# Key and attention-output transposes as pairs of 64-row tiles beside the scores, in a cosformer and mixture-of-experts block

## The chip, the cores and the metric

One core of one Trainium2 chip runs the whole program in one launch. The metric is the device time of that core in microseconds. The kernel is written engine by engine: each engine has its own list of instructions and waits on semaphores that other engines raise.

## What is computed

The input is x, 2048 tokens of 128 numbers. The reference, cut to what matters here:

```python
# x: (1, 2048, 128); 16 heads of 64
n = layernorm(x)
Q, K, V = n @ Wq + bq, n @ Wk + bk, n @ Wv + bv
Qp, Kp = relu(Q), relu(K)
Qc, Qs = Qp * cos, Qp * sin        # angle = pi / (2 * 2048) * token
Kc, Ks = Kp * cos, Kp * sin
# token by token, for each head (a causal linear attention):
S_cos += Kc outer V;  S_sin += Ks outer V;  z_cos += Kc;  z_sin += Ks
out = (Qc @ S_cos + Qs @ S_sin) / max(Qc . z_cos + Qs . z_sin, 1e-6)
x = x + out @ Wo + bo
n = layernorm(x)
# eight experts, the best two for each token, 128 -> 512 -> 128 with gelu
x = x + sum over the two experts of softmax weight * expert(n)
```

## The kernel before

The 2048 tokens are cut into 16 tiles of 128 tokens. Four tiles (`SC`) make one group, and the groups `i` = 0 to 3 (`NS` = 4) run one after another, each as a **front** and an **attention**; behind the last one comes the stage of the experts with 39 blocks.

**The front** (`front`, L1064) computes, with the normed tokens turned so that features lie on partitions, 16 blocks (`block(j)`: eight for keys, eight for queries; three matmuls each, L1054 to L1056) and eight halves of the values (`values(m)`, after the blocks named in `V_AT`). ScalarE takes each block out of PSUM with a relu into `kT` or `qT` (L570). VectorE takes each half of the values out (L712) and writes it twice into `vcs`, times cosine and sine (L716). Between these VectorE also does small steps of the group before: the second layer norm (L789 to L808), and the choice of the two experts (`best_two`, L817 to L838). Then it masks the first scores (`masked(i, 0)`, L751), behind `best_two` in its order and ahead of the last half of the values.

`kT` holds two heads of 64 features on 128 partitions for eight pairs of heads. The keys are needed with tokens on partitions as well (`kn`), for the update of the state. So the front also has eight **key jobs** (`keys(m)`, L1089): each turns four 128x128 squares of `kT` into PSUM bank 5 (L1099), and ScalarE copies the bank to `kn` (L561). `K_AT` says ahead of which block each job stands; the last one stands behind `values(7)`. There are 4 groups x 8 jobs x 4 = 128 such transposes.

**The attention** (L1262) walks over eight pairs `p` of head groups (two pairs for each tile). For each p TensorE does `scores(i, p)` (L1135: eight matmuls with 64 rows each, the two halves of the rows in two PSUM banks), then `outputs(i, p - 1)`: `before` (L1152: queries against the state, 64 rows each, 64x128 tiles) and `within` (L1173 and L1180, 128x64 tiles). An ordinary fp32 matmul of this kernel shows in the trace as two records with a weight load each, a transpose as one. VectorE masks the scores (`masked`) and takes state and outputs away (`taken`, L761 and L767) once ScalarE has copied the sums (`out_sums`, L598). TensorE waits in `scores(p)` for the mask of p-1 (`am_ok`), and in `before(n)` for `tcs_ok` of group n-2.

When a tile is complete, VectorE makes the reciprocal of the denominator (L774), GpSimd divides (`normalise`, L432) into `on`, TensorE turns `on` (`turn_out`, L1193, eight 128x128 transposes, banks 6 and 7, L1200), ScalarE copies to `oT` (L553), and `project` (L1209) multiplies by Wo into bank 7; VectorE adds that to the residual (`residual`, L779). `turn_out` of tiles 0, 1, 2 stands behind `outputs` at p = 3, 5, 7; that of tile 3 stands in the next front (behind block 3), for the last group in the stage of the experts.

Banks 6 and 7 also hold other things for a while: the gate's logits (bank 7, `gate`, L1222, read at L817), the ranks (bank 6, read by `places`, L854), and in the last attention the table of blocks (`blocks_before`, `block_table`, `match_blocks`, `table`) and the first rows for the experts (`first_rows`, `turn_y`).

## Time and profile before

| what | value |
|---|---|
| median of three runs | 376.09 us (376.0 to 377.35) |
| profiled execution, its own time | 377.03 us |
| its span, first to last instruction | 375.2 us |
| granted TensorE clock, mean over the span | 0.985 |
| TensorE busy | 351.7 us (94%) |
| VectorE / ScalarE / GpSimd busy | 65% / 42% / 35% |

A matmul's record lasts longer than the step to the next one, since matmuls are pipelined. The price of a piece of TensorE work is therefore read from starts to starts in the timeline, not from record lengths. In the timeline one row merges consecutive records of one kind: start, length, what, count, and in brackets the idle time of the engine ahead of it with who ended it.

### The profile page before, as it was taken

How to read it: one execution, taken by the hardware profiler on the slowest of the kernel's cores; microseconds unless marked ns; L12 is line 12 of the kernel's file. 1: busy time of each engine (PE TensorE's matmuls, PEld its weight loads, DVE VectorE, ACT ScalarE, POOL GpSimd, SP SyncE). 2: the span in 40 equal slices, each digit the busy share in tenths (PEclk: the TensorE clock that was granted, in tenths of full speed). 3: DMA queues.
4: the chain of work that ended last, by engine and by line, in shares of the span. 5: the costliest groups of instructions: out<-in, count | busy, mean ns of one | idle time of the engine just before them, and what ended most of it. 6: DMA issues, size and time to landing. Idle time of an engine off the chain costs nothing.

```text
span 375.2 us, 10993 instructions
## 1 busy us (share of the span) xinstructions
PE 351.7 (94%) x4125; PEld 319.0 (85%) x4125; DVE 244.9 (65%) x774; ACT 156.5 (42%) x369; POOL 130.1 (35%) x130
## 2 busy tenths in 40 slices
PE   7999999999999999999999999999899999999920
PEld 7877999888899988889898888999789899999910
DVE  4889665768966566896646679866656554444515
ACT  4773231467222146622214672212345555555510
POOL 4022522212086320207732030455037675444530
PEclk9999999999999999999999999999999999999985
DMA  7941530531001000000100005300646677667129
GB/s 254 309 206 40 229 136 10 210 128 52 9 24 48 18 2 1 0 9 27 41 17 9 3 0 145 98 27 26 171 126 191 186 206 213 187 192 192 35 60 282
DMA packets 32773, 38.65 MB, mean 103 GB/s; under 512 B 4140, under 2 KB 25025, under 8 KB 31697
## 3 DMA queue, kind: packets, MB, share of 16 engines
q1 hardware_dynamic: 27248, 31.90, 27.5%
q0 software_dynamic: 2272, 4.46, 3.5%
q10 hardware_dynamic: 3200, 1.58, 1.4%
q8 instruction: 34, 0.56, 0.6%
q14 instruction: 19, 0.15, 0.1%
HBM read 22.91 MB, written 15.47 MB: 102 GB/s over the span
## 4 chain that ended last, share of the span: by engine, by line
PE 82%; DVE 5%; DMA 5%; issue 3%; POOL 1%; ACT 1%; SPq 1%; ACTq 0%; DVEq 0%; POOLq 0%
PE ps L1135 9%; PE ps L1173 9%; PE ps L1359 8%; PE ps L1344 8%; PE ps L1152 7%; PE ps L1180 7%; PE ps L1209 7%; PE ps L1054 6%; PE ps L1056 5%; PE ps L1055 5%; PE ps L1200 4%; PE ps L1099 3%; DMA zin<-zbuf 2%; PE ps L1331 1%; DMA ident<-c_ident 1%
## 5 line engine op out<-in xcount | busy, mean ns | idle before, releaser
L598 ACT ACTIVATE os<-ps 128x260 f32<-128x260 f32 x64 | 24.9, 389 | 99.8 <-PE ps L1180 99.8
L639 ACT ACTIVATE hT<-ps,b1t 128x128 f32<-128x128 f32 x156 | 44.6, 369 | 38.6 <-PE ps L1344 38.6
L474 POOL DMA_INDIRECT ybuf<-yr,slot x32 | 31.9, 997 | 69.4 <-DVE yr L846 31.7
L432 POOL TENSOR_TENSOR on<-tcs,rden 128x1024 f32<-128x1024 f32 x16 | 30.4, 1903 | 65.0 <-DVE rden L774 65.0
L512 POOL DMA_INDIRECT zbuf<-z,tokens x39 | 38.0, 975 | 31.1 <-DVE z L997 25.6
L761 DVE TENSOR_TENSOR state<-ps,state 128x260 f32<-128x260 f32 x64 | 27.4, 428 | 32.4 <-ACT os L598 30.1
L751 DVE TENSOR_TENSOR am<-ps,pair 128x1024 f32<-128x1024 f32 x32 | 38.7, 1208 | 9.3 <-issue 6.7
L1359 PE MATMUL ps<-w_sb,hT 128*128 x312 | 43.1, 281 | 0.6 <-DVE zs L993 0.4
L1344 PE MATMUL ps<-xb,w1b 128*128 128x128 f32 x312 | 42.3, 278 | 0.0
L1173 PE MATMUL ps<-vcs,am 128*64 128x65 f32 x1024 | 42.2, 225 | 0.0
L1173 PEld LDWEIGHTS ps<-vcs,am 128*64 128x64 f32 x1024 | 36.8, 137 | 3.9
L1180 PE MATMUL ps<-vcs,kn 128*64 128x130 f32 x512 | 39.5, 275 | 0.0
L1359 PEld LDWEIGHTS ps<-w_sb,hT 128*128 128x128 f32 x312 | 37.8, 191 | 1.9 <-issue 1.4
L1135 PE MATMUL ps<-qT,kT 64*128 64x128 f32 x512 | 37.2, 284 | 1.0 <-DVE am L751 0.9
L1344 PEld LDWEIGHTS ps<-xb,w1b 128*128 128x128 f32 x312 | 37.9, 192 | 0.0
L1135 PEld LDWEIGHTS ps<-qT,kT 64*128 64x128 f32 x512 | 31.2, 187 | 6.9 <-issue 6.2
L716 DVE TENSOR_SCALAR vcs<-os,cs 128x512 f32<-128x512 f32 x64 | 32.6, 552 | 1.1
L1152 PE MATMUL ps<-state,qT 64*128 64x130 f32 x480 | 33.3, 277 | 0.0
L1209 PE MATMUL ps<-wo_sb,oT 128*128 128x128 f32 x256 | 31.6, 278 | 0.0
L712 DVE TENSOR_TENSOR os<-ps,bv_all 128x512 f32<-128x512 f32 x32 | 22.0, 689 | 14.6 <-PE ps L1056 14.6
L1209 PEld LDWEIGHTS ps<-wo_sb,oT 128*128 128x128 f32 x256 | 29.8, 192 | 1.7 <-issue 1.4
L1152 PEld LDWEIGHTS ps<-state,qT 64*128 64x128 f32 x480 | 30.2, 187 | 0.8 <-issue 0.7
(121 smaller groups left out, 590.0 us busy)
## 6 DMA issues: line engine op xcount, KB each, us to landing
w1b<-in_L_ffn_w SPq DMA_DIRECT2D x39, 256.0 KB, 2.9
ybuf<-blank SPq DMA_DIRECT2D x8, 1152.0 KB, 4.6
yb<-ybuf SPq DMA_DIRECT2D x39, 72.0 KB, 2.9
w_sb<-in_L_ffn_w SPq DMA_DIRECT2D x8, 256.0 KB
x_sb<-in_L_attn_x SPq DMA_DIRECT2D x4, 256.0 KB, 5.2
pair<-c_pair SPq DMA_DIRECT2D x16, 64.0 KB, 2.3
zin<-zbuf SPq DMA_DIRECT2D x4, 256.0 KB, 4.8
zin<-zbuf ACTq DMA_DIRECT2D x4, 256.0 KB, 5.3
```

The lines of the kernel that those rows point to most:

```text
L474: pool.indirect_dma_start(ybuf, bass.IndirectOffsetOnAxis(ap=slot[:, k, c:c + 1], axis=0), yr[:, k, c, :], None).then_inc(y_out[u], 16)
L512: pool.indirect_dma_start(zbuf, bass.IndirectOffsetOnAxis(ap=tokens[:, b:b + 1], axis=0), z[:, b % ZR, :], None, bounds_check=2 * T - 1, o ...
L639: act.activation(hT[:, b % 2, f, :], ps[:, b % 2 * 2 + f // 2, f % 2 * P:f % 2 * P + P], ACT.Gelu, bias=b1t[:, b % XR, f:f + 1]).then_inc( ...
L716: last = dve.tensor_scalar(vcs[:, m // 2, (m % 2) * 8:(m % 2) * 8 + 8, s, 0:DH], vb[:, m % 2, :].rearrange("p (h d) -> p h d", d=DH), cs4[ ...
L751: dve.tensor_tensor(am[:, p % 2, :, :, :], ps[:, 0:2, :].rearrange("p r (q t) -> p r q t", t=P), pair[:, c, None, None, :].broadcast_to([P ...
L1135: last = mm(ps[:, r, b * P:(b + 1) * P], kT[rows, of, c * P:(c + 1) * P], qT[rows, of, c * P:(c + 1) * P], start=True, stop=True)
L1152: mm(ps[:, 2 + 2 * (n % 2) + r, 0:2 * CS].rearrange("p (s b v) -> p b s v", s=2, b=2)[:, q, :, :], qT[rows, 2 * g + q, c * P:(c + 1) * P], ...
L1173: mm(ps[t:t + 64, 2 + 2 * (n % 2) + r, q * VW:q * VW + VW], am[:, n // 2 % 2, r, (2 * g + q) % (PH // 2), t:t + 64], vcs[:, c, g * GH + 2 ...
L1180: last = mm(ps[64 * r:64 * r + 64, 2 + 2 * (n % 2) + q, 2 * CS:3 * CS], kn[:, c, (2 * g + q) * P + r * DH:(2 * g + q) * P + (r + 1) * DH], ...
L1209: last = mm(ps[:, 7, at:at + D], oT[:, c % 2, pr, :], wo_sb[:, pr, :], start=(pr == 0), stop=(pr == NP - 1))
L1344: last = mm(ps[:, b % 2 * 2 + f // 2, f % 2 * P:f % 2 * P + P], w1b[b % WR][:, f * P:(f + 1) * P], xb[:, b % XR, :], start=True, stop=True ...
L1359: last = mm(ps[:, z_bank(b), 0:D], hT[:, b % 2, f, :], w, start=(f == 0), stop=(f == FB - 1))
```

## The change

`turn_out` and the key jobs use 64x128 row tiles in place of whole 128x128 squares. A transpose of 64 partitions by 128 columns has 64 columns of the identity as its moving side. Two of them, on partitions 0 to 63 and 64 to 127, stand in pairs and write different banks.

- `turn_out(c)`: 16 half transposes in eight pairs (tokens 0 to 63 into bank 6, 64 to 127 into bank 7). It moves behind `scores` at p = 4, 6, 8, ahead of `outputs(p - 1)`; at p = 8 there are no scores. For tile 3 its place is kept. The wait for the residual (`x2_ok`) now stands ahead of both banks.
- `keys(i, c)`: one job for each tile, 16 half transposes in eight pairs. Tile 0 is turned at the end of the front, behind `scores(i, 0)` (banks 5 and 7, behind a wait for `lg_ok` when bank 7 held logits); tiles 1, 2, 3 inside the attention behind `scores` at p = 2, 3, 5 (banks 6 and 7). The copies on ScalarE follow: still eight of 512 columns for each group, two at the end of the front and six in the attention, ahead of `out_sums(2p - 2)`.
- New or moved waits of TensorE are in the diff. On VectorE, `residual`, and in the last group `match_blocks` and `table`, move ahead of `masked` of the same p.
- In the last group, `block_table` moves from p = 6 to the end of p = 5, and `first_rows` with `turn_y` from ahead of `outputs(7)` to between its `before` and its `within`.

```diff
+KEYS_AT = {2: 1, 3: 2, 5: 3}
+TURN_AT = {4: 0, 6: 1, 8: 2}
+def key_bank(c, r):
+    return 5 + 2 * r if c == 0 else 6 + r
...
 # ScalarE, attention
-                    if g == 2 and c >= 1:
-                        turn_out(i, c - 1)
+                    if n % 2 == 0 and n // 2 + 1 in TURN_AT:
+                        turn_out(i, TURN_AT[n // 2 + 1])
+                    if n % 2 == 0 and n // 2 + 1 in KEYS_AT:
+                        keys(i, KEYS_AT[n // 2 + 1])
                     out_sums(i, n)
...
 # VectorE, attention
-                    masked(i, p)
                     if p % 2 == 1 and p > 4:
...
+                    masked(i, p)
+                    if tail and p == 1:
+                        places(i - 1)
...
 # TensorE, end of the front
                 scores(i, 0)
+                if tail:
+                    pe.wait_ge(lg_ok, i)
+                keys(i, 0)
                 values(V_JOBS - 1)
-                keys(K_JOBS - 1)
...
+            def keys(i, c):
+                for pr in range(NP):
+                    for r in range(2):
+                        rows = slice(HT * r, HT * r + HT)
+                        last = pe.transpose(ps[:, key_bank(c, r), pr * DH:pr * DH + DH], kT[rows, pr, c * P:(c + 1) * P],
+                                            ident[rows, rows])
...
                 for n in (2 * p, 2 * p + 1):
                     if not opening:
                         before(i, n)
+                if i == NS - 1 and p == PAIRS - 1:
+                    pe.wait_ge(oT_ok, i * 2 * SC + 2 * (SC - 2) + 1)
+                    first_rows()
+                    pe.wait_ge(oT_ok, i * 2 * SC + 2 * (SC - 1))
+                    turn_y(i, 7)
                 for n in (2 * p, 2 * p + 1):
                     within(i, n, opening)
...
             def turn_out(i, c):
                 pe.wait_ge(on_ok, i * SC + c + 1)
-                for half in range(2):
-                    if half == 1 and c >= (1 if i == NS - 1 else 2):
-                        pe.wait_ge(x2_ok, i * SC + c)
-                    for q in range(4):
...
+                if c >= (1 if i == NS - 1 else 2):
+                    pe.wait_ge(x2_ok, i * SC + c)
+                for pr in range(NP):
+                    for k in range(2):
+                        rows = slice(HT * k, HT * k + HT)
+                        last = pe.transpose(ps[:, 6 + k, pr * HT:pr * HT + HT],
+                                            on[rows, c % 2, 2 * pr:2 * pr + 2, :].rearrange("p h d -> p (h d)"),
+                                            ident[rows, rows])
...
 # TensorE, attention, behind scores(i, p)
+                    if p in KEYS_AT:
+                        if p == 2 and tail:
                             pe.wait_ge(cnt_ok, i + 1)
+                        if p == 3:
+                            pe.wait_ge(kn_ok, i * K_JOBS + 4)
+                        if p == 5:
+                            pe.wait_ge(oT_ok, i * 2 * SC + 2)
                         if p == 5 and i == NS - 1:
                             pe.wait_ge(match_ok, 1)
+                            pe.wait_ge(x2_ok, i * SC + 1)
+                        keys(i, KEYS_AT[p])
+                    if p in TURN_AT:
+                        if p < PAIRS:
+                            pe.wait_ge(kn_ok, i * K_JOBS + (6 if p == 4 else 8))
+                        if p == 6 and i == NS - 1:
+                            pe.wait_ge(tab_ok, 1)
...
+                        turn_out(i, TURN_AT[p])
+                    outputs(i, p - 1, opening=not tail and p <= 2)
+                    if p == 5 and i == NS - 1:
+                        pe.wait_ge(kn_ok, i * K_JOBS + K_JOBS)
+                        block_table(0)
```

## Rows read from the trace of the kernel before

**Rows 1.** The page, part 1: busy time, share of the span, instructions.

```profile
PE 351.7 (94%) x4125; PEld 319.0 (85%) x4125; DVE 244.9 (65%) x774; ACT 156.5 (42%) x369; POOL 130.1 (35%) x130
```

**Rows 2.** Waits of TensorE: us in total, times, longest.

```profile
PE ps L1135 <- DVE am L751: 0.9, 1, 0.9
```

**Rows 3.** Groups by line and shape: busy us, mean ns of one record.

```profile
L1099 PE MATMUL ps<-ident,kT 128*128 128x128 f32 x128 | 19.3, 273 | 0.1
...
L1173 PEld LDWEIGHTS ps<-vcs,am 128*64 128x64 f32 x1024 | 36.8, 137 | 3.9
L1099 PEld LDWEIGHTS ps<-ident,kT 128*128 128x128 f32 x128 | 15.7, 142 | 3.4 <-issue 0.5
L1222 PEld LDWEIGHTS ps<-gate_sb,yT 128*128 128x128 f32 x32 | 4.2, 191 | 0.3
```

**Rows 4.** Timeline of TensorE, third front, around two key jobs.

```profile
147.97 0.60 PE L1099 MATMUL ps<-ident,kT 128*128 128x128 f32 x4
...
148.65 0.39 PE L1055 MATMUL ps<-xT_lo,W 128*128 128x512 f32 x1
148.88 0.39 PE L1056 MATMUL ps<-xT_hi,W 128*128 128x512 f32 x1
...
150.49 0.60 PE L1099 MATMUL ps<-ident,kT 128*128 128x128 f32 x4
```

**Rows 5.** Chain of work in order of time, second attention: start, us, what.

```profile
105.02 1.09 PE ps L1135 x16
106.11 0.97 PE ps L1152 x16
107.08 0.62 PE ps L1173 x16
107.69 0.45 PE ps L1180 x8
108.14 0.47 PE ps L1173 x16
...
109.05 1.02 PE ps L1200 x8
110.08 1.09 PE ps L1135 x16
```

**Rows 6.** Timeline of TensorE, fourth front, the gate's matmuls and what follows.

```profile
224.62 0.95 PE L1222 MATMUL ps<-gate_sb,yT 128*128 128x8 f32 x8
225.43 0.64 PE L1099 MATMUL ps<-ident,kT 128*128 128x128 f32 x4
```

**Rows 7.** Timeline of VectorE, third front.

```profile
147.47 0.69 DVE L712 TENSOR_TENSOR os<-ps,bv_all 128x512 f32<-128x512 f32 x1 [0.62 <-PE ps L1056]
...
149.99 0.69 DVE L712 TENSOR_TENSOR os<-ps,bv_all 128x512 f32<-128x512 f32 x1 [0.41 <-PE ps L1056]
...
155.94 0.69 DVE L712 TENSOR_TENSOR os<-ps,bv_all 128x512 f32<-128x512 f32 x1 [0.70 <-PE ps L1056]
...
158.46 0.69 DVE L712 TENSOR_TENSOR os<-ps,bv_all 128x512 f32<-128x512 f32 x1 [0.92 <-PE ps L1056]
...
161.94 1.22 DVE L751 TENSOR_TENSOR am<-ps,pair 128x1024 f32<-128x1024 f32 x1
```

**Rows 8.** Timeline of VectorE, first front: its last idle time and the first mask.

```profile
19.83 0.69 DVE L712 TENSOR_TENSOR os<-ps,bv_all 128x512 f32<-128x512 f32 x1 [0.92 <-PE ps L1056]
...
31.21 1.21 DVE L751 TENSOR_TENSOR am<-ps,pair 128x1024 f32<-128x1024 f32 x1
```

**Rows 9.** Timeline of ScalarE, last attention: one copy of turned outputs.

```profile
253.60 1.09 ACT L553 ACTIVATE oT<-ps 128x512 f32<-128x512 f32 x2 [0.19 <-PE ps L1200]
```

**Rows 10.** Timeline of TensorE, end of the last attention.

```profile
264.23 1.09 PE L1200 MATMUL ps<-ident,on 128*128 128x128 f32 x8
...
266.73 0.33 PE L1259 MATMUL ps<-ident,yb 128*128 128x128 f32 x1 [0.83 <-DMA yb<-ybuf]
...
267.20 1.17 PE L1152 MATMUL ps<-state,qT 64*128 64x130 f32 x16
```

More of the change, by code:

```diff
@@ L50 @@
 K_JOBS = 2 * SC
+HT = P // 2
 GROUPS = SC * NG
@@ L916, in attention @@
                             residual(i, 0, 2)
-                    if tail and p == 1:
-                        places(i - 1)
                     if i == NS - 1 and p == 5:
@@ L1087, in values @@
                            ).then_inc(v_ps, 1)
-                def keys(m):
-                    c, half = K_ORDER[m]
-                    if m == 0:
-                        pe.wait_ge(big_ok, i * QK_JOBS + NP // 2)
-                    elif half == 1:
-                        pe.wait_ge(big_ok, i * QK_JOBS + NP)
-                    if m >= 1:
-                        pe.wait_ge(kn_ok, i * K_JOBS + m)
-                    for q in range(4):
-                        last = pe.transpose(ps[:, 5, q * P:(q + 1) * P], kT[:, half * 4 + q, c * P:(c + 1) * P], ident[:])
-                    last.then_inc(kn_ps, 1)
                 for j in range(QK_JOBS):
@@ L1104, in front @@
                         pe.wait_ge(tcs_ok, i * GROUPS)
-                    if j in K_AT:
-                        keys(K_AT[j])
                     block(j)
@@ L1118, in front @@
                 scores(i, 0)
+                if tail:
+                    pe.wait_ge(lg_ok, i)
+                keys(i, 0)
                 values(V_JOBS - 1)
-                keys(K_JOBS - 1)
                 if tail:
@@ L1137, in scores, with keys @@
                 last.then_inc(sc_ps, 1)
+            def keys(i, c):
+                for pr in range(NP):
+                    for r in range(2):
+                        rows = slice(HT * r, HT * r + HT)
+                        last = pe.transpose(ps[:, key_bank(c, r), pr * DH:pr * DH + DH], kT[rows, pr, c * P:(c + 1) * P],
+                                            ident[rows, rows])
+                        if pr == NP - 1:
+                            last.then_inc(kn_ps, 1)
             def before(i, n):
@@ L1143, in before @@
                     pe.wait_ge(v_add, i * V_JOBS + V_JOBS)
-                    pe.wait_ge(kn_ok, i * K_JOBS + K_JOBS)
+                    pe.wait_ge(kn_ok, i * K_JOBS + 2)
                 if n >= 2:
@@ L1162, in within @@
                     pe.wait_ge(v_add, i * V_JOBS + V_JOBS)
-                    pe.wait_ge(kn_ok, i * K_JOBS + K_JOBS)
+                    pe.wait_ge(kn_ok, i * K_JOBS + 2)
                 if opening and n >= 2:
@@ L1194, in turn_out @@
                 pe.wait_ge(on_ok, i * SC + c + 1)
-                for half in range(2):
-                    if half == 1 and c >= (1 if i == NS - 1 else 2):
-                        pe.wait_ge(x2_ok, i * SC + c)
-                    for q in range(4):
-                        pr = half * 4 + q
-                        last = pe.transpose(ps[:, 6 + half, q * P:(q + 1) * P],
-                                            on[:, c % 2, 2 * pr:2 * pr + 2, :].rearrange("p h d -> p (h d)"),
-                                            ident[:])
-                    last.then_inc(oT_ps, 1)
+                if c >= (1 if i == NS - 1 else 2):
[6 more added lines that the diff above has]
+                                            ident[rows, rows])
+                        if pr == NP - 1:
+                            last.then_inc(oT_ps, 1)
             def project(i, c):
@@ L1287, in attention @@
                             blocks_before(0)
-                        if i == NS - 1 and p == 6:
-                            pe.wait_ge(tab_ok, 1)
                         if i == NS - 1 and p == PAIRS:
```

29 lines of the change are left out of this document (6 added, 23 removed).

## The prediction, made before the change was built

> **What bounds the kernel now.** I read the busy times first, then who waited for whom, then the timelines of TensorE and VectorE side by side through one front, one attention and the last attention. TensorE is busy 94% of the span, and no other engine comes near [rows 1]. The list of its waits has hardly anything in it: the largest one inside the groups is a single 0.9 us at the first mask of the first front [rows 2]. So from the second group on every piece of TensorE work lies on the path, and a piece that gets shorter shortens the kernel, unless an engine close behind TensorE then becomes the last. The question is therefore twofold: what a transpose costs in either form, and who stands close behind TensorE in the stretch that loses work. Over the span VectorE is busy only 65% [rows 1], but in the fronts it has almost no holes: in the third front, from the second layer-norm step to the first mask, only three holes, 0.41, 0.70 and 0.92 us [rows 7]; in the first front none at all after 19.83 [rows 8].
>
> **Price of the whole transposes.** From one key job to the next but one piece in the third front it is 2.52 us (147.97 to 150.49). In it stand nine projection matmuls with 0.23 us from start to start, 2.10 us. So a job of four costs 0.42 us and one whole transpose 0.105 us [rows 4]. A `turn_out` in the attention costs 1.03 us (109.05 to 110.08) [rows 5], against 8 x 0.105 = 0.84 in a run of whole tiles; the other 0.19 us I take as the price of one more change of tile form (128x64 to 128x128 to 64x128 instead of straight from the first to the last). All in all 128 transposes of keys [rows 3] and as many of outputs.
>
> **Price of the pairs, t for a job of eight pairs.** No half transpose is in the trace, so I bound it. From below: half the moving columns at the whole price, 0.105 / 2 a pair, t = 0.42. Nearest row: `within` in its second half, 16 records with 65 moving columns on pairs of 64-column tiles, in 0.47 us, 0.029 us a record [rows 5]; t = 0.46 to 0.47. That row tiles overlap in pairs is seen in the scores: 16 records with 128 moving columns in 1.09 us, 0.068 each, form change included, which is well below 0.105 for the same columns in a whole tile [rows 5]. From above, by the weight load: the gate's eight records have only 8 moving columns and still take 0.81 us (224.62 to 225.43), so an ordinary load of 128 columns takes 0.10 us [rows 6], and with two loads side by side t = 0.81. Further above, if the halves follow one another at the whole price: 16 x 0.105, t = 1.68. I take t = 0.46. The load's record decides: the transposes' loads last 142 ns, as long as those of 64 columns (137), not as the gate's (191), though all 128 columns are loaded [rows 3]; so their load is the short kind, and `within` shows what pairs with short loads cost.
>
> The Trainium skill speaks against this choice: "TensorE: Matmul & The Clock Gate", section "LDWEIGHTS (loading the stationary operand)", says that a load's time follows its columns and not its rows, so a half transpose, still 128 columns wide, would load as long as a whole one. The gate's row agrees with it for ordinary loads; the 142 ns of the transposes' loads speak against applying it here. By that rule the sum would be that of the second rival below.
>
> **The fronts.** Eight key jobs leave each front (8 x 0.42 = 3.36 us of TensorE), one job t comes back, and the front's `turn_out` becomes t plus a form change in and out, 0.66 in place of 0.84. TensorE alone would gain about 3.1 us. But VectorE sets the end. From the third value half (147.47) to the seventh (158.46) it runs 10.99 us with 2.03 us of holes, 8.96 of work [rows 7]. The third half itself comes earlier by one key job and the `turn_out`'s 0.2: 0.6 us. Without holes the seventh half is taken 0.6 + 2.03 = 2.6 us earlier; TensorE's part of it (six key jobs and 0.2: 2.7) is just in time. After that VectorE works without a hole (multiplications, `best_two`, mask) to the end of the first mask, and `scores(1)` waits for it. So a tail front gains 2.6 us less a little for semaphores: 2.55, three times, **7.7 us**. `keys(0)` at its end costs nothing there: TensorE has 0.5 us to spare before `scores(1)`; without this cover it costs t, 0.46, each. The wait for `lg_ok` stands before `keys(0)`, with `values(7)` and the ranks queued behind it; VectorE copies the logits right after the seventh half, while `scores(0)` runs for 1.1 us, so I cost it at nothing (a tenth or two if late, inside the same 0.5). In the **first front** VectorE is without a hole from 19.83 to the mask at 31.21 [rows 8], and TensorE waits 0.9 us for it already [rows 2]. Only the two key jobs ahead of the fourth half count: **0.8 us**; the rest turns into waiting.
>
> **The attentions.** In each, three `turn_out` change from 1.03 to t and three key jobs of t come in: 3 x (1.03 - 2t), with t = 0.46 a gain of 0.33, four times **1.3 us**. The moved copies of the keys on ScalarE: the present copies of two banks start 0.19 us after the transposes and last 1.09 [rows 9]; the sums that stand behind them are due after `before` and one `within`, 0.97 + 0.62 + 0.45 = 2.04 us [rows 5]. 0.76 us to spare, so I cost them at nothing; without that cover each of the 24 jobs would hold up `out_sums`, `taken` and then `before`. The waits on `kn_ok`, `oT_ok`, `cnt_ok`, `on_ok` and the earlier `x2_ok` each ask for something that ended a `scores` or an `outputs` before, with the half transposes and `outputs` queued behind. The wait for GpSimd's division gets looser, as tile 0 is turned a `scores` later. `residual` ahead of `masked` on VectorE waits for `project`, which TensorE ended before the very scores that `masked` needs: nothing.
>
> **The last attention.** `turn_out(1)` now waits for the table, with `outputs(5)` behind it; VectorE writes the table after both `taken` of p = 5, so one `scores` (about 1 us) has to cover what an `outputs` covered. Bounds 0 to 1 us; I take 0.4. The other way `first_rows` behind `before` hides the copy and the load that it waited for: up to 0.83 + 0.25 us of the stretch 264.23 to 267.20 [rows 10], though `before(15)` now meets `taken(13)`; I take 0.4. Together nothing. The table is finished earlier, but SP's first loads also wait for the scattered rows, whose place is kept. `turn_out(3)` behind it saves 0.84 - 0.66 and a little: **0.3 us**.
>
> **Sum.** 7.7 + 0.8 + 1.3 + 0.3 = 10.1 us; as a function of t: 24t - 21.2. The profiled execution took 377.03, 0.9 above the median; 10.1 less is 366.9 for it, and **366.0** beside the median of 376.09. The experts' stage starts earlier as a whole and keeps its own pace, for TensorE is the bound there too.
>
> **The rivals.**
> First, ScalarE's copies become late. They are written in pieces of 64 numbers instead of in one run. If two copies took 2.2 us instead of 1.09, they would pass the 2.04 us by 0.33, 24 times: 8 us, 374. It decides from 1.85 us. For it: no copy of this shape is in the trace. Against it: the 0.76 us to spare, and the sums themselves are not awaited at once. Partly right it gives 369 to 373.
> Second, the pair is bound by its loads, t = 0.81 as by the gate's row: 24 x 0.81 - 21.2 = -1.8, 374.3, and up to 375.5 where a form change adds 0.05 a job. This is no measurable change, or just below it.
> Third, on the slower side: two half transposes don't overlap at all and each costs what a whole one costs, 0.105: t = 1.68, +19 us, 395. It decides where 24t passes 21.2, at t = 0.88, 0.055 us a half one after another or 0.11 a pair. For it: no transpose in row pairs is in the trace. Against it: the scores' and the queries' records in the same form overlap [rows 5].
>
> **How the numbers follow.** Forecast (t from 0.42 to 0.6, fronts bound by VectorE): 0.70, 363 to 369. Late copies: 0.11, 369 to 374. Bound by loads: 0.11. Serial halves: 0.08. The range 362.5 to 373 takes the forecast's bounds (t = 0.42 gives 365.0, and the 0.55 us of each tail front that I gave to VectorE would bring 363.3) and most of the late copies, and leaves out the loads' case and the serial one. About 0.5%, 1.9 us, is what a measurement here tells from no change: faster (below 374.2) 0.81, within 0.11, slower 0.08.
>
> **What would show it.** Eight pairs in 0.42 to 0.6 us between `scores` and `before` in the timeline; at 0.8 the loads bind. Fronts shorter by 2.5 us, with a new wait of TensorE for the mask (L751) of up to 0.5 us at the end of each, and of over 2 us in the first. Copies of keys on ScalarE of about 0.55 us each, ended before the sums. Attentions shorter by about 0.3 us. The prediction is wrong if a job takes over 0.7 us, if TensorE waits for `tcs` or ScalarE in the attention, or if the fronts shrink by far less than 2 us.

## The result, and the profile after

The changed kernel takes 371.54 us (median of 4, 370.48 to 373.75) against 376.72 for the kernel before, measured beside it: a ratio of 0.9872 with a 95% interval of 0.9844 to 0.990, or 1.3% faster. A later set of the same kernel (`after_again`, expected near 371.5) gave 372.85 (median of 6, 371.01 to 373.95), ratio 0.9894 [0.987, 0.9919]. The forecast was 366.0. The direction was right and the time lies in the range, but the gain is 5.2 us where 10.1 were worked out: half of it is missing. The time also lies above the 363 to 369 of the forecast itself, in the part of the range that was kept for late copies on ScalarE. These did not come, as is shown below, so it is luck that the time fell inside the range.

The profiled execution took 372.44 us, its span is 370.6. From its page: busy time of the engines, the granted clock in 40 slices, and the shares of the chain that ended last. PE is TensorE, PEld its weight loads, DVE VectorE, ACT ScalarE and POOL GpSimd.

```profile
PE 342.9 (93%) x4381; PEld 309.7 (84%) x4381; DVE 244.5 (66%) x774; ACT 157.3 (42%) x369; POOL 129.9 (35%) x130
...
PEclk9998999999999999999999999999999999999975
...
PE 74%; DVE 12%; DMA 4%; issue 4%; POOL 2%; ACT 2%; SPq 1%; ACTq 0%; DVEq 0%; POOLq 0%
```

TensorE is busy 8.8 us less than in [rows 1] although the span shrank by only 4.6. The rest became waiting. The chain says the same: VectorE holds 12% of it, where it held 5% before. And one slice near the start of the clock row reads 8. The list of TensorE's waits (who waited <- for whom, us in total, times, longest) stands against a single 0.9 inside the groups in [rows 2]:

```profile
PE ps L1128 <- DVE am L757: 3.6, 5, 2.0
...
PE ps L1137 <- issue: 0.9, 1, 0.9
...
PE ps L1208 <- POOL on L438: 0.7, 1, 0.7
PE ps L1155 <- DVE tcs L773: 0.5, 1, 0.5
...
PE ps L1208 <- issue: 0.3, 1, 0.3
```

L1128 is the scores, L1137 the keys, L1208 `turn_out`, L1155 `before`, L757 the mask; `issue` means that the profile shows nothing that was waited for. The one wait of `before` in this list stands in the last attention (262.89); those of the groups before it lie inside merged rows. Where in the program this lies is read from the starts of landmarks on TensorE (first block of a front, second scores of a group, first hidden matmul of the experts), the same in both timelines:

| stage, us | before | after | forecast | measured |
|---|---|---|---|---|
| first front, to `scores(1)` | 22.97 | 22.31 | -0.8 | -0.66 |
| fronts 2, 3, 4, each | 26.18 | 23.72 | -2.55 | -2.46 |
| attention 1 | 38.19 | 40.26 | -0.33 | +2.07 |
| attention 2, 3, each | 40.18 | 40.53 | -0.33 | +0.35 |
| attention 4, to the experts | 42.49 | 44.20 | -0.33 | +1.71 |
| start, and the experts' stage with tile 3 | 112.64 | 111.60 | -0.3 | -1.04 |

The last row moves by as much between kernels that don't touch it (the experts' stage 102.15 to 103.67, the start 9.2 to 11.3), so nothing is read into it. The fronts came out as forecast. The attentions were to give 1.3 us and took 4.5: the whole error is there.

**The price of a job.** Timeline of TensorE in the second attention of the changed kernel (start, us, what):

```profile
108.61 1.16 PE L1128 MATMUL ps<-qT,kT 64*128 64x128 f32 x16
109.60 0.66 PE L1208 MATMUL ps<-ident,on 64*128 64x64 f32 x16
110.09 1.12 PE L1155 MATMUL ps<-state,qT 64*128 64x130 f32 x16
...
113.12 1.16 PE L1128 MATMUL ps<-qT,kT 64*128 64x128 f32 x16
114.11 0.66 PE L1137 MATMUL ps<-ident,kT 64*128 64x64 f32 x16
114.61 1.12 PE L1155 MATMUL ps<-state,qT 64*128 64x130 f32 x16
```

From start to start a job of eight pairs takes 0.49 to 0.50 us (109.60 to 110.09, 114.11 to 114.61), 0.062 a pair. So t = 0.50, where 0.46 was taken. The step from scores to scores is 4.51 with either job in it, where the kernel before has 5.06 with a whole `turn_out` [rows 5] and, by the same trace, 3.96 to 4.04 without.

**The end of a front.** The third one, TensorE:

```profile
156.50 1.16 PE L1128 MATMUL ps<-qT,kT 64*128 64x128 f32 x16
...
157.50 0.66 PE L1137 MATMUL ps<-ident,kT 64*128 64x64 f32 x16
...
159.87 1.16 PE L1128 MATMUL ps<-qT,kT 64*128 64x128 f32 x16 [0.36 <-DVE am L757]
```

`keys(0)` stands inside the time that TensorE had to spare, and what is left of that, 0.36 us, is the new wait for the mask. The mask itself starts 22.36 us after the front's first block (158.51), against 24.82 in [rows 7]. In the first front the same wait is 2.01 us, where it was 0.93.

### The profile page after: what moved, and what is told of

Same layout as the page of the kernel before. It is cut to its first block, busy times and chain, and to the rows that moved or that the text cites. A ratio compares the mean times of both kernels' runs of the same rounds, so it can differ in the third digit from the quotient of the medians.

```text
span 370.6 us, 11502 instructions
## 1 busy us (share of the span) xinstructions
PE 342.9 (93%) x4381; PEld 309.7 (84%) x4381; DVE 244.5 (66%) x774; ACT 157.3 (42%) x369; POOL 129.9 (35%) x130
## 2 busy tenths in 40 slices
DMA packets 32774, 38.68 MB, mean 104 GB/s; under 512 B 4139, under 2 KB 25024, under 8 KB 31696
## 3 DMA queue, kind: packets, MB, share of 16 engines
q10 hardware_dynamic: 3200, 1.58, 1.4%
## 4 chain that ended last, share of the span: by engine, by line
PE 74%; DVE 12%; DMA 4%; issue 4%; POOL 2%; ACT 2%; SPq 1%; ACTq 0%; DVEq 0%; POOLq 0%
PE ps L1357 9%; PE ps L1372 8%; PE ps L1176 8%; PE ps L1128 7%; PE ps L1218 7%; PE ps L1183 7%; PE ps L1155 6%; PE ps L1060 5%; PE ps L1062 5%; PE ps L1061 5%; DVE vcs L722 2%; PE ps L1344 2%; PE ps L1208 2%; DMA zin<-zbuf 2%; DVE am L757 2%
## 5 line engine op out<-in xcount | busy, mean ns | idle before, releaser
L1176 PE MATMUL ps<-vcs,am 128*64 128x65 f32 x1024 | 42.9, 227 | 0.0
L1372 PE MATMUL ps<-w_sb,hT 128*128 x312 | 41.9, 278 | 0.6 <-DVE zs L999 0.5
L1128 PE MATMUL ps<-qT,kT 64*128 64x128 f32 x512 | 37.3, 285 | 3.6 <-DVE am L757 3.6
L1183 PE MATMUL ps<-vcs,kn 128*64 128x130 f32 x512 | 40.4, 279 | 0.0
L1128 PEld LDWEIGHTS ps<-qT,kT 64*128 64x128 f32 x512 | 31.3, 188 | 9.9 <-issue 8.8
L757 DVE TENSOR_TENSOR am<-ps,pair 128x1024 f32<-128x1024 f32 x32 | 38.6, 1207 | 0.9 <-PE ps L1128 0.8
L1155 PE MATMUL ps<-state,qT 64*128 64x130 f32 x480 | 34.5, 279 | 0.9 <-DVE tcs L773 0.5
L1155 PEld LDWEIGHTS ps<-state,qT 64*128 64x128 f32 x480 | 29.9, 188 | 1.7 <-DVE tcs L773 1.7
L574 ACT ACTIVATE kT<-ps,bcols 128x512 f32<-128x512 f32 x32 | 21.6, 689 | 19.8 <-PE ps L1062 19.7
```

The source lines that it names most:

```text
L757: dve.tensor_tensor(am[:, p % 2, :, :, :], ps[:, 0:2, :].rearrange("p r (q t) -> p r q t", t=P), pair[:, c, None, None, :].broadcast_to([P ...
L1128: last = mm(ps[:, r, b * P:(b + 1) * P], kT[rows, of, c * P:(c + 1) * P], qT[rows, of, c * P:(c + 1) * P], start=True, stop=True)
L1155: mm(ps[:, 2 + 2 * (n % 2) + r, 0:2 * CS].rearrange("p (s b v) -> p b s v", s=2, b=2)[:, q, :, :], qT[rows, 2 * g + q, c * P:(c + 1) * P], ...
L1176: mm(ps[t:t + 64, 2 + 2 * (n % 2) + r, q * VW:q * VW + VW], am[:, n // 2 % 2, r, (2 * g + q) % (PH // 2), t:t + 64], vcs[:, c, g * GH + 2 ...
L1183: last = mm(ps[64 * r:64 * r + 64, 2 + 2 * (n % 2) + q, 2 * CS:3 * CS], kn[:, c, (2 * g + q) * P + r * DH:(2 * g + q) * P + (r + 1) * DH], ...
L1372: last = mm(ps[:, z_bank(b), 0:D], hT[:, b % 2, f, :], w, start=(f == 0), stop=(f == FB - 1))
```

## The experiments

The theory formed from this: t = 0.50 explains 24 x 0.04 = 0.96 of the 5.8 us that the attentions are off; the rest is four waits or their consequences. (1) After the 2.01 us wait of the first front the granted clock falls, and the first attention runs slowly for a while, 1.6 us. (2) At p = 8 `before(15)` now meets a wait that the long `turn_out(2)` had covered, 0.48 in each of the first three groups. (3) and (4) In the last attention VectorE stands still behind GpSimd at p = 3 and p = 5, ahead of the mask: 0.60 and 1.09. The rivals blame the half transposes themselves or their places. Line numbers are those of each kernel, so they are shifted by some lines in places. Medians of the kernel before, measured beside the experiments, lie at 376.55 to 376.91. The fronts behind the first one are called tail fronts.

### A filler in the first front's wait

The slow stretch of attention 1: timeline of TensorE in the changed kernel, then its busy time by stretch (us, busy and count for PE, PEld, DVE, ACT, POOL, then granted clock, DMA share, GB/s).

```profile
31.63 1.16 PE L1128 MATMUL ps<-qT,kT 64*128 64x128 f32 x16 [2.01 <-DVE am L757]
...
36.14 1.08 PE L1128 MATMUL ps<-qT,kT 64*128 64x128 f32 x12
```

```profile
32.00:35.50 3.50, 3.50 (x59) 3.38 (x58) 2.66 (x6) 0.39 (x1) 0.00 (x0) 0.65 0.05 16
...
35.50:39.00 3.50, 3.50 (x71) 3.10 (x68) 2.19 (x4) 1.73 (x4) 0.00 (x0) 0.86 0.83 337
39.00:60.00 21.00, 21.00 (x427) 19.64 (x424) 13.99 (x30) 8.27 (x19) 7.04 (x7) 1.00 0.31 123
```

The step from `scores(1)` to `scores(2)` is 4.51 us, 3.07 in the kernel before. Mean clocks of 0.65 and 0.86 are full speed and the lower of the two levels, 1.2 GHz, mixed (0.51 from 33 to 36 us). The edit fills the wait with eight matmuls that no one reads (work that the kernel itself uses ahead of its start), in a bank that is free:

```diff
                 if tail:
                     ranks(i - 1)
+                else:
+                    keep_busy(8, 6)
...
```

> The changed kernel with eight matmuls on zeros into bank 6 put in front of the first group's scores(1), where TensorE waits 2.01 us for the first mask. Theory 'idle time costs the clock': the granted clock stays at 1.00 from 30 to 40 us (it was 0.51 from 33 to 36), the step from scores(1) to scores(2) of the first attention goes from 4.51 to about 3.1 us, the one after it from 3.70 to 3.56, and the time is about 370.8 us or 1.6 below the disturbed profile of the changed kernel (372.4). Rival 'the half transposes at 28 us bring the clock down': they stand in the same place here, so the clock falls again and the step stays at 4.5.

Measured (`e1_filler`): 371.02 (370.45 to 372.19), ratio 0.9842 [0.9816, 0.9868]. The same stretches of this kernel:

```profile
32.00:35.50 3.50, 3.26 (x67) 2.92 (x68) 3.27 (x7) 0.40 (x2) 0.00 (x0) 1.00 0.02 5
35.50:39.00 3.50, 3.50 (x82) 3.26 (x82) 2.65 (x6) 2.15 (x5) 0.00 (x0) 1.00 0.72 287
```

The wait shrinks to 0.24, the clock stays at 1.00, the first step is 3.07 again and attention 1 takes 38.68: 1.58 less. The front is as long as before (22.33), since VectorE sets its end. So in these two profiles the waiting itself was free and the clock after it was not. The medians differ by less, 0.5 us, and their intervals overlap: by their mean clocks, the clock does not fall in every execution. The four of the changed kernel took 372.44, 373.75, 370.48 and 370.65 us at mean clocks of 0.977, 0.976, 0.981 and 0.982.

### The first front without the statistics of two groups

VectorE computes the first layer norm's statistics of groups 1, 2 and 3 in the first front. Those of 2 and 3 move into the first attention, and GpSimd's roots of them with them:

```diff
-                    if not tail and 4 <= m < NS + 3:
-                        norm1_stats(m - 3)
+                    if not tail and m == 4:
+                        norm1_stats(1)
...
+                    if i == 0 and p in (3, 4):
+                        norm1_stats(p - 1)
...
```

> The changed kernel with the layer-norm statistics of token groups 2 and 3 taken out of the first front on VectorE (two pieces of 1.47 us) and put behind the state updates of p = 3 and p = 4 in the first attention. Theory 'VectorE sets the end of the first front': scores(1) comes 2.8 us after the start of scores(0) plus its own work, the wait for the mask falls from 2.01 us to under 0.3, the two waits of 0.22 and 0.57 for the value halves vanish, the clock stays at 1.00, in all 2.8 + 1.6 = 4.4 us less: 368 us. Rival 'another engine stands right behind it' (ScalarE's relus): the wait shrinks by less than 1 us and the time by under 1.5 us.

Measured (`e2_stats_late`): 369.21 (369.03 to 372.9), ratio 0.9831 [0.9774, 0.9887]; 368 was expected. The first front takes 20.14, 2.17 less, of some 2.8 us that left VectorE there. So VectorE set the end of that front. Now TensorE does, for the first mask waits 0.30 us for the scores:

```profile
28.10 1.23 DVE L763 TENSOR_TENSOR am<-ps,pair 128x1024 f32<-128x1024 f32 x1 [0.30 <-PE ps L1136]
```

TensorE's wait for the first mask is gone and the clock stays at 1.00. Attention 1 takes 39.59, not 38.68: GpSimd takes one of the moved roots right ahead of a division (48.46 and 49.43), and the step that holds `turn_out(1)`, which needs this division, is 9.62 in place of 8.72.

### Whole transposes again at p = 8

```diff
+                if i < NS - 1 and c == SC - 2:
+                    for pr in range(NP):
+                        last = pe.transpose(ps[:, 6 + pr // 4, pr % 4 * P:pr % 4 * P + P],
+                                            on[:, c % 2, 2 * pr:2 * pr + 2, :].rearrange("p h d -> p (h d)"), ident[:])
...
```

> The changed kernel with tile 2 of the groups 0 to 2 turned by eight whole transposes again, at its new place (p = 8, without scores ahead). Theory 'at p = 8 the shorter job only uncovers the wait for the state sums': the job gets about 0.5 us longer three times, the wait inside before() shrinks by as much, from scores(7) to the next front stays 9.8 us (it was 9.86 with whole tiles before the change, 9.81 after), and the time does not move (under 0.4 us). Rival, the prediction's sum: each of the three jobs counts in full, 3 x 0.5 = 1.6 us more and 10.3 us for the stretch.

Measured (`e3_whole_at_p8`): 372.49 (370.45 to 374.61), ratio 0.9886 [0.9844, 0.9929]. Its executions spread like those of the changed kernel, so the medians, 0.95 us apart, decide nothing here; the stretch does. From `scores(7)` to the next front it takes 9.86, against 9.81 in the changed kernel and 9.86 in the kernel before. `turn_out(2)` costs 1.02 in this form:

```profile
130.26 1.09 PE L1211 MATMUL ps<-ident,on 128*128 128x128 f32 x8
131.28 1.17 PE L1159 MATMUL ps<-state,qT 64*128 64x130 f32 x16
```

This is 0.45 us more than in the changed kernel (66.05 to 66.62), and the stretch is only 0.05 longer. What the half form saves at this place is waited away at once. The changed kernel's rows at p = 8 of the first group, of TensorE, of the weight loads of `before`'s second half, and of VectorE's step that takes outputs 13:

```profile
66.05 0.71 PE L1208 MATMUL ps<-ident,on 64*128 64x64 f32 x16
66.62 1.56 PE L1155 MATMUL ps<-state,qT 64*128 64x130 f32 x16
68.11 0.69 PE L1176 MATMUL ps<-vcs,am 128*64 128x65 f32 x16
...
67.46 0.53 PEld L1155 LDWEIGHTS ps<-state,qT 64*128 64x128 f32 x8 [0.31 <-DVE tcs L773]
...
66.94 0.47 DVE L773 SCALAR_TENSOR_TENSOR tcs<-os,cs,ps 128x260 f32<-128x260 f32 x1
```

`before` takes 1.49 us there and 1.05 where nothing holds it up (110.09 to 111.14), 0.44 of the 0.48 that the stretch lost: in its second half it waits until VectorE has taken outputs 13 (until 67.41). At the other p a `scores` of 1 us stands between; at p = 8 there is none, only `turn_out`. In the kernel before, `before` took 1.09 at this place (132.25 to 133.34): the whole `turn_out` covered the wait.

### The last attention's table steps, reordered

VectorE has a few tiny steps of the experts' table ahead of masks. Its rows in the last attention, first VectorE, then GpSimd (POOL), then TensorE:

```profile
234.77 1.75 DVE L882 SCALAR_TENSOR_TENSOR ex<-nq,small,free 128x2 fp32r<-128x2 f32 x1
236.44 1.21 DVE L757 TENSOR_TENSOR am<-ps,pair 128x1024 f32<-128x1024 f32 x1
...
244.69 0.15 DVE L891 SCALAR_TENSOR_TENSOR early<-ps,ex 128x2 f32<-128x2 f32 x1
244.88 1.25 DVE L894 TENSOR_TENSOR free<-free,early 128x2 f32<-128x2 f32 x1
...
246.20 1.21 DVE L757 TENSOR_TENSOR am<-ps,pair 128x1024 f32<-128x1024 f32 x1
```

```profile
234.60 1.90 POOL L438 TENSOR_TENSOR on<-tcs,rden 128x1024 f32<-128x1024 f32 x1 [0.71 <-DVE rden L780]
...
244.21 1.90 POOL L438 TENSOR_TENSOR on<-tcs,rden 128x1024 f32<-128x1024 f32 x1 [0.71 <-DVE rden L780]
```

```profile
237.70 1.16 PE L1128 MATMUL ps<-qT,kT 64*128 64x128 f32 x16 [0.53 <-DVE am L757]
...
246.38 0.71 PE L1137 MATMUL ps<-ident,kT 64*128 64x64 f32 x16 [0.91 <-issue]
```

L882 and L894 touch two numbers a row and take 1.75 and 1.25 us. Both end when GpSimd's division ends: 234.77 + 1.75 = 236.52 and 234.60 + 1.90 = 236.50; 244.88 + 1.25 and 244.21 + 1.90, 246.13 and 246.11. L891, between them, reads PSUM for one input and takes 0.15. The Trainium skill, "SBUF — State Buffer", section "Who interferes with whom", says that a VectorE instruction with two inputs in SBUF contends with a GpSimd instruction that reads SBUF, and calls such contention an exclusive lock; the trace agrees with these numbers. The mask behind each step is late by that much, and TensorE with it: `scores(4)` by 0.53, and `keys(3)`, which asks for the table's match (L895), by 0.91. The stand-still at p = 3 is no child of the change (the kernel before has one of 1.75 us at 239.84), but there a `turn_out` stood between it and the scores. The one at p = 5 is new: in the kernel before the same step came behind the mask and behind the end of the division (250.75), and took 0.16 us:

```profile
251.68 0.16 DVE L888 TENSOR_TENSOR free<-free,early 128x2 f32<-128x2 f32 x1
```

There TensorE also asked for the match an `outputs` later, at `turn_out(1)` and not at `keys(3)`.

First only VectorE's order is changed. `full_blocks` goes behind the mask of p = 3, and the update of `free` (L894) from ahead of the match to behind the mask of p = 5:

```diff
+                    if i == NS - 1 and p == 3:
+                        full_blocks(0)
+                    if i == NS - 1 and p == 5:
+                        early_out(0)
...
-                    if i == NS - 1 and p == 2:
-                        full_blocks(0)
```

> The changed kernel with two small steps of VectorE in the last attention put later: full_blocks(0) behind the mask of p = 3 instead of ahead of it, and the update of the free blocks (1.25 us while GpSimd divides) behind the match and the mask of p = 5. Theory 'small steps on VectorE that read only SBUF stand still until GpSimd has ended its division, and now stand ahead of what TensorE waits for': the wait of scores(4) (0.53) goes to under 0.1 and the one of keys(3) (0.91 in the list) to under 0.2, about 1.3 us less in the last attention (44.2 to 42.9). Rival 'the match itself stands still too' (it also reads two SBUF tiles): keys(3) waits as long as now, only 0.5 us are gained.

Measured (`e4_table_order`): 370.23 (369.98 to 374.91), ratio 0.9831 [0.9804, 0.9858]. The step from `scores(3)` to `scores(4)` fell from 5.11 to 4.51, as expected; that at p = 5 only from 5.82 to 5.69, and attention 4 takes 43.36 where 42.9 was expected: there the rival was right. VectorE and GpSimd of this kernel:

```profile
246.11 1.39 DVE L893 SCALAR_TENSOR_TENSOR match<-small,ps,ex 128x17 f32<-128x17 f32 x1
247.42 1.21 DVE L757 TENSOR_TENSOR am<-ps,pair 128x1024 f32<-128x1024 f32 x1
```

```profile
245.57 1.90 POOL L438 TENSOR_TENSOR on<-tcs,rden 128x1024 f32<-128x1024 f32 x1 [0.71 <-DVE rden L780]
```

Now the match stands still, until 247.50 (the division ends at 247.47). It has one input in PSUM and two in SBUF, 0.23 us without company. So the order on VectorE alone was not the cause at p = 5. The division beside it is left, and the next run moves it.

### GpSimd's division behind the match

`full_blocks` as above, `free` where it was, and one wait more on GpSimd in the last group:

```diff
                 pool.wait_ge(rden_ok, i * SC + c + 1)
+                if i == NS - 1 and c == 1:
+                    pool.wait_ge(match_ok, 1)
...
```

> The changed kernel with full_blocks(0) behind the mask of p = 3, and GpSimd's division of tile 1 in the last group held back until the match is written (TensorE needs that division only at p = 6). Theory 'VectorE's small steps with two SBUF inputs stand still until GpSimd's division has ended': the match is done 0.5 us after residual(0), the wait of keys(3) falls from about 0.8 to under 0.2 us, the step from scores(5) to scores(6) from 5.8 to about 4.9, the last attention from 44.2 (43.4 with the first part alone) to about 42.6; nothing else moves. Rival 'keys(3) waits for the residual or the copies, not the match': the step stays at 5.7.

Measured (`e4b_divide_after_match`): 369.22 (368.97 to 370.26), ratio 0.9801 [0.9768, 0.9833]. VectorE's match and mask, then GpSimd's division:

```profile
242.88 0.24 DVE L897 SCALAR_TENSOR_TENSOR match<-small,ps,ex 128x17 f32<-128x17 f32 x1
243.44 1.22 DVE L759 TENSOR_TENSOR am<-ps,pair 128x1024 f32<-128x1024 f32 x1 [0.33 <-PE ps L1130]
```

```profile
243.27 1.90 POOL L440 TENSOR_TENSOR on<-tcs,rden 128x1024 f32<-128x1024 f32 x1 [1.84 <-DVE match L897]
```

The match takes 0.24 us, the mask behind it waits for the scores, the step at p = 5 is 4.73, with 0.18 of `block_table` in it (5.82 in the changed kernel), and attention 4 takes 42.18, 2.02 less than in the changed kernel. This settles (3) and (4).

It also tells something of (1): here the wait in the first front is 2.0 us as well, but the granted clock of 32 to 39 us is 1.00 and attention 1 takes 38.68. In two more profiles on the same chip (`e5_rows_apart`, `e6_whole_moved`) the wait is 1.7 us and the clock stays too. In the four other profiles with the 2.0 us wait (the changed kernel twice, `e3_whole_at_p8`, `e4_table_order`) it fell; in the six with a wait of at most 0.93 it never did. Four of these six (`e1_filler`, `e2_stats_late`, `e8_all_three`, `e9_block_early`) ran on chips where it fell behind the long wait. In these runs, then, the fall comes only behind the long wait, and not always; whether the chip or the moment decides was not tried.

### GpSimd's opening of the residual behind its first division

If VectorE sets the end of the tail fronts, as the prediction had it, work of GpSimd that slows VectorE there must cost the front time. `open_residual` leaves the front:

```diff
+                    if i >= 1:
+                        rows_paced(i, c)
+                    normalise(i, c)
                     if c == 0:
...
                         open_residual(i)
-                    if i >= 1:
-                        rows_paced(i, c)
-                    normalise(i, c)
```

> The changed kernel with GpSimd's addition of the output bias to the tokens (1.28 us, in the fronts) put behind its first division in each attention. Theory 'VectorE sets the end of the tail fronts, and GpSimd stretches two of its multiplications there from 0.88 to 1.97 us': these take about 0.9 to 1.4 (the copy of 0.61 us still stands beside them), VectorE is ready about 0.6 to 1.1 us earlier, TensorE's wait for the mask (0.36 us) vanishes and the front falls from 23.72 to about 23.3: about 1.2 us in three fronts. Rival 'TensorE sets the end of the front': no change.

Measured (`e7_open_late`): 370.01 (369.57 to 370.66), ratio 0.9817 [0.9786, 0.9847]. The first front takes 21.23, 1.08 less, with a wait of 0.9 and the clock at 1.00. But the tail fronts take 23.69, only 0.03 less, and the wait for the mask stays at 0.37: there the theory fell. VectorE's sixth and seventh value halves, in the third front, have holes ahead of them again:

```profile
150.53 0.69 DVE L718 TENSOR_TENSOR os<-ps,bv_all 128x512 f32<-128x512 f32 x1 [0.62 <-PE ps L1062]
152.63 0.69 DVE L718 TENSOR_TENSOR os<-ps,bv_all 128x512 f32<-128x512 f32 x1 [0.48 <-PE ps L1062]
```

In the tail fronts of this kernel TensorE sets the time up to the seventh value half, and VectorE only from there to the mask. In the changed kernel VectorE has no hole there, and its seventh half starts at the same point of the front (18.87 us behind the first block, 18.85 here): both engines arrive together. The prediction's two sums for that stretch, 2.6 by VectorE and 2.7 by TensorE, were so close that either gave the right number.

### The halves not in pairs

Both loops are swapped, so that eight halves of partitions 0 to 63 come first and then eight of 64 to 127:

```diff
-                for pr in range(NP):
-                    for r in range(2):
+                for r in range(2):
+                    for pr in range(NP):
```

> The changed kernel with the same 16 half transposes of every job in another order: first the eight of partitions 0 to 63, then the eight of 64 to 127, so that neighbours share their rows of the array. Theory 'a pair costs 0.06 us because its two halves run side by side': a job goes from 0.50 to 0.85 or more (16 x 0.053), the steps of 4.51 between scores become about 4.9, the time grows by about 7 us. Rival 'the halves follow one another in any case and are simply short': the job stays at 0.50.

Measured (`e5_rows_apart`), one execution: 377.41. The rows between which a job lies:

```profile
109.94 1.16 PE L1128 MATMUL ps<-qT,kT 64*128 64x128 f32 x16
...
114.74 1.16 PE L1128 MATMUL ps<-qT,kT 64*128 64x128 f32 x16
```

The step is 4.80, 0.30 more than with pairs, so a job costs 0.80: 0.050 us for each half after another, 0.062 for a pair. Half transposes overlap when partitions and banks alternate, but by 0.30 of 0.80 and not by half. This order changes both at once, so which of the two counts is not shown. A single half costs half of a whole one (0.105, [rows 4]), not as much. Without the pairing no gain is left (377.41 against 376.91 for the kernel before).

### Whole transposes at the new places

The places of the change with 128x128 squares, in `keys`, `turn_out` and ScalarE's copies:

```diff
                 for pr in range(NP):
-                    for k in range(2):
-                        rows = slice(HT * k, HT * k + HT)
...
+                    last = pe.transpose(ps[:, 6 + pr // 4, pr % 4 * P:pr % 4 * P + P],
+                                        on[:, c % 2, 2 * pr:2 * pr + 2, :].rearrange("p h d -> p (h d)"), ident[:])
```

> The changed kernel with whole 128x128 transposes in all key and output jobs, everything at its new place. Theory 'only the form makes the new places pay': a job beside the scores costs 0.84 + about 0.2 to 0.35 for two more changes of form, 1.05 to 1.2 us instead of 0.50, the steps of 4.51 become 5.1 to 5.2; five such jobs in each attention are not covered by a wait: 4 x 5 x 0.6 = 12 us more than the changed kernel, slower than before the change by 6. Rival 'the new places alone give the gain': as fast as the changed kernel within 2 us.

Measured (`e6_whole_moved`), one execution: 384.19. The rows of one job and its neighbours:

```profile
112.00 1.16 PE L1127 MATMUL ps<-qT,kT 64*128 64x128 f32 x16
113.09 1.09 PE L1203 MATMUL ps<-ident,on 128*128 128x128 f32 x8
114.11 1.17 PE L1152 MATMUL ps<-state,qT 64*128 64x130 f32 x16
```

Steps are 5.19 in place of 4.51, so a whole job takes 0.68 more of the step than eight pairs. Of this 0.52 is the job itself, 1.02 from start to start (113.09 to 114.11), as behind `outputs` (1.03, [rows 5]). The rest lies in its neighbours: `scores` takes 1.09 where it took 0.99 (108.61 to 109.60), `before` 1.10 where it took 1.05. In a run of whole tiles the job cost 0.84 (8 x 0.105). The fronts take 23.76, as in the changed kernel: their gain is that the key jobs left, not the form. By this one execution the places alone lose some 7 us and the form wins about 12.

### All remedies at once, and one block more

The edits of the second, the fifth and the sixth experiment together; the moved roots go behind the second division.

> The changed kernel with three moves: layer-norm statistics of token groups 2 and 3 out of the first front (their roots on GpSimd behind the second division), the bias addition behind the first division, and the last group's small steps of the table ordered against GpSimd's divisions as in e4b. By the waits seen so far: first front 22.3 to about 20.1, no wait over 0.5 us for a mask and the clock at 1.00 there, first attention 38.7, last attention 42.2 in place of 44.2 or 43.9: about 4 us less than the changed kernel's undisturbed 370.5, 366.5. If something else stands behind these waits (the chain through GpSimd, SP's loads), it stays above 368.5.

Measured (`e8_all_three`): 367.58 (367.11 to 369.22), ratio 0.9772 [0.9749, 0.9794]. The first front takes 19.62, attention 4 42.44. It fell 1.1 us short of its expectation: the steps of p = 5 in attention 1 (5.18 for 4.51) and of p = 4 in attention 4 (6.87 for 6.61) are longer. In both VectorE has a step that now stands beside work of GpSimd and ends with it: L689 takes 0.90 (0.17 alone) and ends at 48.82, a division at 48.80; L887 takes 0.99 (0.22 alone) and ends at 234.28, the moved addition at 234.26. In `e2_stats_late`, with the same statistics at this place but no division beside them, the step that is L689 here took 0.17, and the step of p = 5 was 4.51.

Last, the wait at p = 8 gets something to cover it: the first block of the next front's projection goes ahead of `turn_out(2)`.

```diff
                         if p == PAIRS and i + 1 < NS:
                             pe.wait_ge(xThi_ok, i + 2)
                             pe.wait_ge(xTlo_ok, i + 2)
+                            pe.wait_ge(am_ok, i * PAIRS + PAIRS)
+                            key_or_query(0)
                         turn_out(i, TURN_AT[p])
```

> e8 with the first projection block of the next front (0.70 us of TensorE) pulled ahead of the turning of tile 2 at p = 8, where TensorE otherwise waits about 0.45 us inside before() for the state sums. Theory 'at p = 8 only that wait was uncovered': scores(7) to the next front's second block takes 10.3 us instead of 9.81 + 0.70, about 0.3 us less in each of three groups (0.45 of wait less 0.19 for one more change of form), 0.8 us in all. Rival 'VectorE's chain into the next front sets the pace, not TensorE': no change.

Measured (`e9_block_early`): 366.08 (365.94 to 367.57), ratio 0.9741 [0.9719, 0.9762]; beside the version without it the stretch from `scores(1)` of the first group to the experts falls from 233.92 to 233.14, 0.26 for each of the three groups. `before` now runs through:

```profile
62.52 0.50 PE L1067 MATMUL ps<-xT_hi,W 128*128 128x512 f32 x1
...
63.41 0.71 PE L1220 MATMUL ps<-ident,on 64*128 64x64 f32 x16
63.96 1.11 PE L1167 MATMUL ps<-state,qT 64*128 64x130 f32 x16
65.01 0.69 PE L1188 MATMUL ps<-vcs,am 128*64 128x65 f32 x16
```

The gain is less than the 0.44 waited before, since the block takes 0.89 us at this place (62.52 to 63.41) and 0.70 among other blocks (three steps of 0.23, [rows 4]). This version is 2.6% faster than the kernel before, and 6.8 us faster than the changed one on the same chip (372.85).

## Why the prediction was wrong by half of its gain

**The price of a pair: right, slightly small.** t = 0.50 lies between the bounds, near the row that decided (`within`, 0.47). 24 x 0.04 = 0.96 us of the missing gain. The second rival, by which the loads bind (t = 0.81), fell: loads of half transposes last 139 ns in the records, and even one after another the halves go at 0.050 us each. The rule that the prediction weighed ("TensorE: Matmul & The Clock Gate" of the Trainium skill, section "LDWEIGHTS (loading the stationary operand)": the columns set a load's time) is seen in the records, which are about as long for a half (139 ns) as for a whole (142, [rows 3]); the time that follows from it did not come. The third rival, halves that don't overlap, fell with t = 0.50. It put a half at the price of a whole; the run with the halves apart shows half of that.

**The fronts: right in size, in part by luck.** 7.7 forecast, 7.4 measured for the three tail fronts; 0.8 and 0.66 for the first. `keys(0)` cost nothing there, under the 0.5 us of cover, and the wait for the mask came out at 0.36. That VectorE sets the end holds for the first front, and in the tail fronts from the seventh value half on; up to there, by the sixth experiment, freeing VectorE gains nothing, and the forecast was saved by the two sums being alike.

**ScalarE's copies: right.** Two copies of keys took 1.09 us together (158.19 in the third front, 165.52 in its attention), as long as those in one run [rows 9], and ended 0.94 us before the next sums were due. The first rival fell. (By its own terms copies of 2.2 us would have been late by 0.19 + 2.2 - 2.04 = 0.35 us, not 0.33; nothing hung on it.)

**The attentions: wrong, and all of the error.** Forecast -1.3, measured +4.5; fronts and the rest together came out 0.3 better than forecast in the profiled executions. The difference of 5.8 is t (0.96) and three steps that failed:
- "3 x (1.03 - 2t)" counts the shorter `turn_out(2)` in full, as if nothing stood behind it. The old `turn_out` of 1.03 us was a cover there: at p = 8 there is no `scores`, and `before(15)` waits on `tcs_ok`. The list of waits that "each ask for something that ended a `scores` or an `outputs` before" does not have this one; the prediction saw it for the last attention only ("`before(15)` now meets `taken(13)`"). With 0.53 us less, the stretch of 9.86 was due at 9.33 and took 9.81: 3 x 0.48 = 1.44.
- "Together nothing", for the last attention. The two terms named were near: `turn_out(1)` waits 0.43 us for the table (251.56 instead of 251.13), forecast 0.4, and the end of that attention is 0.7 us shorter (1.0 in most of the other kernels), forecast 0.5 for the `turn_out` and 0.4 for the first rows. What was not named are the steps of the table that VectorE does ahead of its masks, and the wait of `keys(3)` for the match. The stand-still behind GpSimd was in the trace of before, as 1.75 us for two numbers a row. With the `turn_out` gone that had covered it at p = 3, and the match moved ahead of the mask at p = 5, they cost 0.60 + 1.09 = 1.69.
- "The rest turns into waiting", for the first front, costed at nothing. The wait came as foreseen (over 2 us), but the granted clock fell behind it: 1.58 in the profiled execution, nothing in that of `e4b_divide_after_match`.

0.96 + 1.44 + 1.69 + 1.58 = 5.67 of the 5.8. The first three are there in both profiles of the changed kernel. The fall of the clock is too, but `e4b_divide_after_match` has the same wait without it; why it comes in one execution and not in another stays open.

Of what the prediction named as signs, one came true against it: TensorE does wait for `tcs` in the attention. It was written down as what would make the forecast wrong, but no term of the sum held it.

## What to carry to other kernels

When a piece of work on the engine that bounds gets shorter or moves, list for its old place what other engines do meanwhile, down to their smallest steps, and price each wait that it covered; a pattern that holds for seven of eight steps must be read at the eighth too. An idle stretch of TensorE is not free where its granted clock can fall behind it, as in four of five profiles here, so small filler work or an earlier start of real work can be worth more than the wait looks. And a tiny VectorE step whose record is several times longer than its like may be standing still behind someone: look at who ends at the same moment before it is moved.

## What the runs showed of the hardware

- Pairs of 64x128 transposes, with partitions and banks alternating, cost 0.062 us a pair; halves on the same partitions and bank, one after another, 0.050 each; whole ones 0.105 in a run of their kind and 0.128 (1.02 / 8) between pieces of 64-row work, whose neighbours lose another 0.15 us a job. The records, 222 ns for a half and 273 for a whole, show none of that.
- VectorE steps of 2 to 17 numbers a row with two inputs in SBUF took 1.01 to 1.75 us beside GpSimd's division (1.01 is the step of L876 in the fourth experiment), and ended with it within 0.03 us; the same steps alone took 0.10 to 0.24. A step with one tile as input (L689 of `e8_all_three`) took 0.90 beside a division, 0.17 alone.
- After a wait of 2.0 us in the first front the clock granted to TensorE fell to 1.2 GHz in four profiles and stayed at 2.4 GHz in one; with a wait of at most 0.93 us it stayed in all six. What tells them apart is open.
